# Differential attention on one core: the exponential in eight groups of 64 keys, with bias and sum on ScalarE

## The reference

```python
q = (x @ Wq).reshape(b, t, H, HD).transpose(0, 2, 1, 3)      # H = 16, HD = 128; k and v likewise
q1, q2 = (q[..., :HHD], q[..., HHD:])                        # HHD = 64
scores1 = jnp.einsum('bhtc,bhsc->bhts', q1, k1) * SCALE      # SCALE = 1/8; scores2 likewise
scores1 = jnp.where(causal[None, None], scores1, neg_inf)
attn1 = jax.nn.softmax(scores1, axis=-1)
attn2 = jax.nn.softmax(scores2, axis=-1)
lam = jax.nn.sigmoid(lambda_init)[None, :, None, None]
diff_attn = attn1 - lam * attn2
out = jnp.einsum('bhts,bhsd->bhtd', diff_attn, v)
out = out.transpose(0, 2, 1, 3).reshape(b, t, H * HD)
return out @ Wo
```

## Time and profile before

| | |
|---|---|
| median of 3 runs | 894.39 us (891.5 to 895.23) |
| the profiled execution | 895.78 us, span 894.0 us |
| mean granted TensorE clock | 0.911 |
| PE / DVE / ACT / POOL busy | 824.9 / 581.2 / 433.9 / 349.9 us |
| the stage of the heads | about 163 to 296 us of the span |
| L1191, exponential, 16 times | 0.63 us each |
| L1242, subtraction, 16 times | 0.69 to 0.82 us |
| L1248, sum, 16 times | 0.68 us |
| L1254, product, 16 times | 0.69 us, longest 2.82 |

### The profile page before, as it was taken

How to read it: one execution, slowest core, us unless ns; L and a number is a source line. 1 busy time by engine, 2 the same in 40 slices (tenths; PEclk the granted TensorE clock), 3 DMA queues, 4 the chain that set the end, 5 groups by cost and what they waited for, 6 DMA issues and landing times.

```text
span 894.0 us, 15742 instructions
## 1 busy us (share of the span) xinstructions
PE 824.9 (92%) x5725; PEld 646.5 (72%) x5725; DVE 581.2 (65%) x915; ACT 433.9 (49%) x840; POOL 349.9 (39%) x393
## 2 busy tenths in 40 slices
PE   8889997899998799899979999899997999999997
PEld 6523335678787688687658888668996888888886
DVE  6989985686767467788856665466664445454443
ACT  3878884344444345345545665212333445454543
POOL 2288884231321334346701212212222344454442
PEclk8855556999999899999999999998999999999999
DMA  5279894012111132111201111101110233332331
GB/s 173 59 143 168 178 178 92 25 60 78 46 45 39 46 89 82 57 38 54 70 7 36 37 36 42 59 24 48 48 36 24 72 89 89 90 96 87 101 89 47
DMA packets 107062, 64.29 MB, mean 72 GB/s; under 512 B 71921, under 2 KB 94961, under 8 KB 106994
## 3 DMA queue, kind: packets, MB, share of 16 engines
q1 hardware_dynamic: 106994, 63.37, 27.8%
HBM read 46.05 MB, written 0.52 MB: 52 GB/s over the span
## 4 chain that ended last, share of the span: by engine, by line
PE 60%; DVE 16%; POOL 10%; issue 6%; ACT 5%; DMA 2%; DVEq 0%; SPq 0%; POOLq 0%; ACTq 0%
PE ps L158 15%; PE ps L160 14%; PE ps L159 14%; POOL pt L753 6%; PE ps L1591 3%; DVE x L1362 2%; PE ps L1887 2%; PE ps L1888 2%; PE ps L1571 2%; PE ps L1083 1%; POOL nb L760 1%; DVE u_lo L1833 1%; PE ps L1094 1%; DVE hh L1354 1%; ACT h_hi L1346 1%
## 5 line engine op out<-in xcount | busy, mean ns | idle before, releaser
L272 POOL TENSOR_TENSOR wa_lo<-raw,wa_hi 128x512 fp32r<-128x512 f32 (+1 forms) x112 | 136.4, 1218 | 199.8 <-ACT wa_hi L263 199.4
L272 POOL TENSOR_TENSOR wb_lo<-raw,wb_hi 128x256 fp32r<-128x256 f32 (+1 forms) x112 | 94.0, 840 | 252.0 <-ACT wb_hi L263 252.0
L158 PE MATMUL ps<-xt_hi,wa_hi 128*128 128x512 f32 x336 | 136.4, 406 | 1.6 <-DVE soft L1237 0.9
L160 PE MATMUL ps<-xt_hi,wa_lo 128*128 128x512 f32 x336 | 133.8, 398 | 0.0
L159 PE MATMUL ps<-xt_lo,wa_hi 128*128 128x512 f32 x336 | 133.7, 398 | 0.0
L1354 DVE TENSOR_TENSOR hh<-sg,ps 128x512 f32<-128x512 f32 x56 | 38.5, 688 | 73.1 <-PE ps L160 69.2
L263 ACT ACTIVATE wa_hi<-raw 128x512 fp32r<-128x512 f32 (+1 forms) x112 | 63.4, 566 | 45.8 <-PE ps L160 32.9
L856 ACT ACTIVATE kres<-ps,nb,qs 128x1024 int16<-128x1024 f32 x64 | 77.0, 1204 | 17.5 <-POOL nb L760 17.1
L1356 DVE TENSOR_TENSOR h_lo<-hh,h_hi 128x512 fp32r<-128x512 f32 x56 | 58.7, 1048 | 39.9 <-ACT h_hi L1346 39.9
L989 DVE TENSOR_REDUCE nm<-ps 128x1 f32<-128x1024 f32 x64 | 78.0, 1223 | 9.4 <-PE ps L679 6.9
L158 PEld LDWEIGHTS ps<-xt_hi,wa_hi 128*128 128x128 f32 x336 | 64.2, 191 | 15.8 <-issue 3.0
(11 more groups left out here) (290 smaller groups left out, 1879.6 us busy)
## 6 DMA issues: line engine op xcount, KB each, us to landing
raw<-w_l1f SPq DMA_DIRECT2D x44, 256.0 KB, 2.7
raw<-w_l1f SPq DMA_DIRECT2D x44, 128.0 KB, 2.0
raw<-w_l0a SPq DMA_DIRECT2D x16, 256.0 KB, 2.8
raw<-w_l1p SPq DMA_DIRECT2D x32, 128.0 KB, 2.1
raw<-w_l1x SPq DMA_DIRECT2D x32, 128.0 KB, 2.1
raw<-w_l1a SPq DMA_DIRECT2D x16, 256.0 KB, 2.6
raw<-w_l0f SPq DMA_DIRECT2D x12, 256.0 KB, 2.8
raw<-w_l0a SPq DMA_DIRECT2D x16, 128.0 KB, 2.1
```

Source lines behind the costliest of these rows:

```text
L158: nc.tensor.matmul(o, a[0], b[0], start=start, stop=False, **kw)
L160: return nc.tensor.matmul(o, a[1], b[0], start=False, stop=stop, **kw)
L272: nc.gpsimd.tensor_tensor(lo[:, u, 0:w], raw[:, u, cols], hi[:, u, 0:w].bitcast(F32), ALU.subtract).then_inc(done, 1)
```

## The change

In each head the maximum of each group is no longer subtracted from the scores. VectorE takes the negated maximum and scales its eight columns by 1/8; ScalarE computes the exponential in eight instructions, one per group of 64 keys, with that column as bias and with the sum of the group as second output (`accum_out`). The sum on VectorE goes. The count of semaphore steps per head falls from 5 to 4.

```diff
@@ l0a_act
-                nc.scalar.activation(pr[:, u, :], st, ACT.Exp, scale=T ** -0.5).then_inc(l0["e"], 1)
+                for g in range(8):
+                    last = nc.scalar.activation(pr[:, u, g * T:(g + 1) * T], st[:, g * T:(g + 1) * T], ACT.Exp, bias=mx[:, g:g + 1], scale=T ** -0.5, accum_out=sm[:, g:g + 1])
+                last.then_inc(l0["e"], 1)
@@ l0a_dve
-        STEPS0 = 5
+        STEPS0 = 4
...
-                nc.vector.tensor_reduce(mx[:], groups(st), AX.X, ALU.max).then_inc(l0["dve"], 1)
+                nc.vector.tensor_reduce(mx[:], groups(st), AX.X, ALU.max, negate=True).then_inc(l0["dve"], 1)
                 dve.wait_ge(l0["dve"], c.up())
-                nc.vector.tensor_tensor(groups(st), groups(st), wide(mx[:], 8, T), ALU.subtract).then_inc(l0["sh"], 1)
+                nc.vector.tensor_scalar(mx[:], mx[:], T ** -0.5, None, ALU.mult).then_inc(l0["sh"], 1)
...
                 dve.wait_ge(l0["e"], h + 1)
-                nc.vector.tensor_reduce(sm[:], groups(pr[:, u, :]), AX.X, ALU.add).then_inc(l0["dve"], 1)
-                dve.wait_ge(l0["dve"], c.up())
                 nc.vector.reciprocal(rc[:], sm[:]).then_inc(l0["dve"], 1)
```

## The result

| | before | changed | ratio, 95% interval |
|---|---|---|---|
| median of the runs on one chip | 892.94 us (890.06 to 895.23) | 908.59 us (907.01 to 911.79) | 1.0191 (1.0154 to 1.0228) |
| profiled execution, its span | 895.78, 894.0 us | 908.61, 906.8 us | |

The change makes the kernel 15.65 us slower by the medians and 12.8 us by the two profiled executions. The ratio is not the quotient of the two medians (1.0175); its interval lies wholly above 1. The page's line of busy time says where the loss does not come from: VectorE lost 15 us of work, ScalarE gained 32 and is still busy for only half of the span.

A forecast was written before the change was run, and what follows sets the result against it. TensorE was taken as the bound, with softmax bounding heads 0 to 2, 13 to 15 and held-up 3 and 7. Terms 2.50+2.13+2.92+1.18+1.23+1.6 made +11.6 us: 907.4 on the profile's scale, 906.0 on the median's, range 899 to 914.

The forecast's parts named there:

- eight exponentials, from first start to last read's end: ScalarE, each head: eight steps of 0.33 us, 2.75 in all, against 0.63 for the single exponential.
- heads 0, 1, 2: First heads, softmax-bound: later `dd` delays TensorE's transposes by 0.87, 0.84 and 0.79 us, sum 2.50.
- head 3, and head 4 behind it: Late block delays head 3's exponentials and the value split holds `dd`: +2.13 us; slow clock behind it as before.
- head 7, and head 8 behind it: Late block and value split put head 7's `dd` at 11.16 us: +2.92; head 8's slow clock kept.
- steady heads 5, 6, 9 to 12: TensorE-bound heads: `dd` still ready before the transposes, load loop 7.63 us under 7.89; no loss.
- heads 13, 14: Late heads where softmax has no slack: transposes at 6.58 us against 5.40 and 5.35, +1.18 and +1.23.
- last head to the end of the stage: Head 15: the feed-forward block's load is issued after `wb_lo`, which ends later: +1.6 us.
- the rival in which they do not shrink: ScalarE's exponential steps each stay 0.39 us despite fewer columns: +5.8 us more, 911.8 in all; chance 0.18.
- the rival of the uncontested port: `wb_lo` does not hold VectorE's L1254 and the value split follows `dd`: +5.6 us, 900.0; chance 0.20.
- The rival on the other side: Value split falls behind `dd` in heads 3 and 7, removing waits and slow clock: −0.8 us, 893.6; chance 0.08.
- The slow clock: TensorE's slow stretches in heads 4 and 8 (0.85 granted, 9.23 us) stay as they are.
- The block's time from the end of `wb_lo` to landing: Loads for heads 3 and 7: block lands 4.99 and 6.01 us after the preceding head's `wb_lo`, as before the change.

The follow-up runs named there:

- all moves: Changed kernel with block ahead of value weights, `wb_hi` ahead of exponentials, factor 1/8 in query copy, value split moved before key copy: 888.84 us, ratio 0.9986.
- the run with the block ahead: Changed kernel with SyncE issuing the next query and key block ahead of the value weights: 902.80 us, ratio 1.0123.

## Why the prediction was right

The forecast was slower, 906.0 with 899 to 914; the time is 908.59. Against the kernel before it was +11.6 us, and +15.65 was measured. The signs that it named appeared: steps of 0.33, waits for `dd` in heads 0 to 3, 7 and 13 to 15 and none in 9 to 12, L1254 longer beside `wb_lo`, and `wa_hi` waits of 4.06 and 3.27 us in heads 3 and 7.

| term | predicted | first pair of profiles |
|---|---|---|
| eight exponentials, from first start to last read's end | 2.75 | 2.77 |
| end of `dd` after the mask addition, heads 0 and 1 | 6.08 | 6.10, 6.11 |
| the same with `wb_lo` in the way, heads 2, 13, 14 | 6.52 | 6.54, 6.53, 6.53 |
| heads 0, 1, 2 | +0.87, +0.84, +0.79 | +0.89, +0.87, +1.04 |
| head 3, and head 4 behind it | +2.13, 0 | +3.29, +0.29 |
| head 7, and head 8 behind it | +2.92, 0 | +2.48, +0.59 |
| steady heads 5, 6, 9 to 12 | 0 | 0.0 each |
| heads 13, 14 | +1.18, +1.23 | +1.20, +1.24 |
| last head to the end of the stage | +1.6 | +1.94 |

*ScalarE's steps.* 0.33 was right, and the rival in which they do not shrink (0.39) falls. The Trainium skill, "ScalarE: Activation LUTs", "What ACT_TABLE_LOAD costs", gave 2.01 us for eight with a bias; without the reads they took 2.03, so the page holds for the exponentials, and the accumulator read, which it does not price, is the other 0.74.

*The port.* L1254 took 1.12 to 1.14 us wherever `wb_lo` was beside it, and the run with `wb_hi` ahead of the exponentials freed it (0.69). So the rival of the uncontested port falls. The three parts of the loss (the longer chain, the late block, VectorE held by POOL) overlap and do not add: moving the loads took back 5.4 us of the stage, moving `wb_hi` 8.3, and all moves with the folding 16.8, which includes losses that the kernel before already had.

*The rival on the other side.* "Not slower" wanted the value split out of `dd`'s way. It did not happen by itself, for the reason given (the block's landing). Done by hand it does go: with all moves the stage is at 129.0 and the kernel at 0.9986, near the 893.6 against 894.39 (0.999) that the rival had for this case.

*What was mis-sized.* The slow clock was kept "as they are". In the changed kernel the granted clock of the stage was 0.91, against 0.96 and, in the second profile, 0.97 before; heads 2, 4 and 8 are longer for it (+0.25, +0.29, +0.59). The block's time from the end of `wb_lo` to landing was carried over from the kernel before, and in both heads it came out otherwise. In head 3 it took 5.96 us (186.32 to 192.28) for 4.99, so the exponentials began at s+4.05 and not 3.33. In head 7 it took 5.43 for 6.01, and they began at s+3.63 and not 4.20. The two errors partly cancel in the sum, and that is luck.

And one effect was not in the sum at all. The prediction named as held by POOL the operations with two inputs in SBUF. The small scaling L1244 has one, was costed at 0.17, and is held as well: the loads push POOL's `wa_lo` onto it in some heads, where it took 1.25 to 1.26 (the rows of the run with the block ahead and of the changed kernel's second profile).

Of the 4.05 us between +11.6 and +15.65, 1.2 are left if both profiled executions are compared (907.4 forecast on that scale, 908.61 measured), and there a stage 2.2 us longer than in the sum stands against 1.0 us less outside it. The other 2.8 are the base: the sum was made against a profile that lay 2.84 us above its kernel's median, and whose heads 7, 8 and end held 3.5 us that the second profile of the same kernel does not have. The steps were right; the landing times, the clock and that base were not, and part of the closeness of 906.0 to 908.59 is luck.

## What to carry to other kernels

The exponential split in eight pays its fixed part eight times (0.63 us became 1.28 by the split alone, 2.03 with the bias and 2.77 with the sums). Look at what is queued behind such an operation on its own engine: `dd` came 0.9 us later in head 0, but `wb_lo`, and with it the next load, 1.6 us later in head 14. Here the order of the loads and on ScalarE decided over four times as much as the change itself in the best order (all moves with the folding: 16.8 us of the stage; the change with all moves: 3.7). Before trusting a term that contains a race between two engines or a slow clock, take a second profile of the unchanged kernel.

## What was not expected of the hardware

A VectorE operation on 128x8 numbers with one input tensor took 1.25 to 1.30 us when POOL's subtraction had begun 0.02 to 0.06 us earlier, and 0.17 when POOL began 0.04 us later; the scaling by lambda on 128x4 took 2.34 for 0.23 beside the value split. It goes the other way too: in the run with the exponential cut only, the product (L1256 there) began 0.08 us ahead of head 7's value split and kept its 0.69, and the split took 2.82 us for 2.38.

TensorE's granted clock is not the same from one execution to the next: head 8 of the kernel before took 8.85 us at 0.89 in one profile and 7.89 at 1.00 in the other, behind waits of 1.50 and 0.99 us in head 7. The same shows in the unchanged code behind the stage, which took between 590.6 and 598.5 us in the profiles. The longest and the shortest:

```profile
311.09:909.60 598.51, 559.16 (x3488) 472.42 (x3486) 357.42 (x579) 263.19 (x560) 211.61 (x208) 0.97 0.20 58
292.58:883.20 590.62, 551.69 (x3488) 466.22 (x3486) 357.92 (x579) 262.97 (x558) 211.99 (x208) 0.98 0.20 59
```

With the same number of instructions TensorE was busy 7.5 us longer, nearly the whole difference of 7.9, at the lower clock, while VectorE, ScalarE and POOL agree within 0.6. So, as far as these two profiles show, what moves there is TensorE's time under the low clock; what brings it on in one execution and not in another stays open.
